# Two edits to a fused attention and feed-forward layer: attention and its output one head later, and the rotary halves swapped by VectorE instead of by DMA

## The chip, the cores and the metric

One Trainium2 chip, one core. The metric is the device time of one execution in microseconds (us). A profiled execution of the same program gives the trace.

## The reference

Input x is (4, 512, 512): four batches of 512 rows, 512 wide. The weights are integer codes with scales.

```
a = layernorm(x)
q, k, v = a @ Wq, a @ Wk, a @ Wv          # Wq = (codes - 8) * scales, 32 query heads, 8 key/value heads, 128 wide
q, k = rope(q), rope(k)                    # (even*cos - odd*sin, odd*cos + even*sin)
p = softmax(q k^T / sqrt(128) + causal mask)
x = x + layernorm((p v) @ Wo)              # each key/value head serves 4 query heads
x = x + layernorm(ffn(layernorm(x)))       # silu(gate) * up, then down; 1376 hidden
```

## The kernel before

All products run on TensorE (PE) in pairs or triples of float16 parts: a float32 value is written as high + low, and high*high, high*low and low*high are summed in PSUM. VectorE (DVE), ScalarE (ACT) and GpSimd (POOL) make those parts; the DMA queue that SyncE (SP) feeds turns matrices of parts by DMA transposes.

**Units and slots.** The attention part is 32 units (8 key/value heads times 4 batches), `UNITS`, and each unit is 4 slots, one per query head; head number n counts from 0 to 127. In a slot every engine goes through a list written out by hand in its own `unit` function, and the engines meet only at semaphores. In slot n, PE does, in this order (`unit` of the tensor block): `attend(n - 1)`, the product of probabilities and values of the head before (lines 843 to 845, 30 matmuls of 128 columns); the scores of head n + 1 in three groups (lines 827 to 829), with output tiles O0, O1, O2 of head n - 2 between them (lines 814 and 815); then the projections for the next unit that the table `FULL` gives this slot (K or Q0 to Q3, lines 790 to 792, 12 matmuls of 512 columns; V, lines 806 to 808, 48 of 128), and O3. So slots 0 and 1 of a unit carry two projections and slots 2 and 3 one.

**The ring.** Projections and output tiles share the four banks of `ps_p`; PE may refill a bank when DVE has emptied it (`bank_free`).

**DVE's slot.** Three times scaled, masked scores with their row minimum (line 1127) and the bias of the exponential (`bias`, line 1136), each followed by the addition of an output tile into y (`add_output`, line 1114); `invert` (line 1141); then `take` for each projection: the product with the sine table into `other` (line 1099) and with the cosine table into `rot` (line 1102), or V's low part (line 1091). Slot 1 has a `dequant` more (line 1058), slot 3 a `w_low` (line 1048).

**The other engines.** Of a rotary piece SP copies the two halves of `other` crosswise into `swap` by two DMAs (`swap_halves`, lines 370 and 371); POOL adds `swap` to `rot` (`rope_add`, line 492) and, after ACT's high part, makes the low one (`rope_low`, line 500). ACT does the exponentials (line 627) and the high parts of probabilities (line 636) and outputs (`o_norm`, lines 644 and 648); POOL their low parts (`p_low`, line 508; `o_low`, line 516). SP's list in a slot is: the swaps of the last slot's pieces, `turn_p_hi(n)`, `turn_p_lo(n)`, `turn_o(n - 1)` with two transposes (lines 395 and 398), then loads. Turned probabilities have two buffers: `turn_p_hi(n)` waits until head n - 2 has been attended (`oq_ps`).

**Around it.** A start makes the first unit's pieces in the order `START`; after unit 1, POOL issues the load of the feed-forward weights (lines 566 and 567); in the last unit the slots have turned rows (Y, X) in place of projections; behind it stand the last heads' attention and output, and then the feed-forward part.

Of the kernel before, what the change touches and what calls it, by code (L numbers as in the profile page):

```python
# [104 lines left out]
def outs_before(U):  # L105

    return HG * KT * U - 2 * KT
# [22 lines left out]


def swaps_landed(V, piece):


    users = BUF_USERS[ROPE_BUF[piece]]
    return 32 * (len(users) * V + users.index(piece) + 1)
# [21 lines left out]
def layer(nc, x, w_codes, w_scales, o_codes, o_scales,  # L158
          gate_t, gate_s, up_t, up_s, down_t, down_s, cos_t, sin_t, ident_in, mask_in, out):
    ctx = ExitStack()  # L160
    with ctx:
# [56 lines left out]
        other = sb("other", [P, 3, S], F32, att)  # L218
# [4 lines left out]
        o_hi = sb("o_hi", [P, S], F16, att)  # L223
        o_lo = sb("o_lo", [P, S], F16, att)
        ot_hi = sb("ot_hi", [P, 2, TT, P], F16, att)
        ot_lo = sb("ot_lo", [P, 2, TT, P], F16, att)
# [6 lines left out]
        inv_sum = sb("inv_sum", [P, 2, TT], F32, att)  # L233
# [44 lines left out]
        other_done = sem("other_done")  # L278
        swap_in = [sem("swap_in0"), sem("swap_in1"), sem("swap_in2")]
# [16 lines left out]
        ot_hi_in = sem("ot_hi_in")  # L296
        ot_lo_in = sem("ot_lo_in")
# [36 lines left out]
        def _(sp):  # L334
# [27 lines left out]
            def swap_halves(V, vpar, piece):  # L362


                buf = ROPE_BUF[piece]
                after(sp, rot_sum, buffer_before(V, piece))
                sp.sem_inc(sp_passed)
                sp.wait_ge(other_done, rope_index(V, piece) + 1)
                sp.sem_inc(sp_passed)
# [18 lines left out]
            def turn_o(n, hp):  # L388


                after(sp, o_ps, (n - 1) * KT)
                sp.sem_inc(sp_passed)
                sp.wait_ge(oq_hid, n + 1)
                sp.sem_inc(sp_passed)
# [21 lines left out]
            swap_halves(0, 0, "K")  # L416
            load_w(4, 0)
            swap_halves(0, 0, "Q0")
            load_w(5, 1)
            swap_halves(0, 0, "Q1")  # L420
            swap_halves(0, 0, "Q2")
# [7 lines left out]
            def unit(U, r, slots=FULL, first=False, more=True, last=False):  # L429
                for h in range(HG):  # L430
                    n = U * HG + h
                    if first and h == 0:
                        swap_halves(0, 0, "Q3")
                    else:
                        for V, vpar, piece, bank, taken in made_before(U, r, h, slots):
                            if piece != "V":
                                swap_halves(V, vpar, piece)
# [21 lines left out]
            unit(UNITS - 1, 1, slots=LAST, more=False, last=True)  # L459
            turn_o(UNITS * HG - 1, 1)  # L460
# [15 lines left out]
        def _(pool):  # L476
# [8 lines left out]
            def rope_add(V, vpar, piece, taken):  # L485
# [4 lines left out]
                pool.wait_ge(swap_in[buf], swaps_landed(V, piece))  # L490
                pool.sem_inc(pool_passed)
# [18 lines left out]
            def o_low(n):  # L510

                after(pool, ot_lo_in, 16 * n)
# [3 lines left out]
                pool.tensor_tensor(o_lo[:, :], o_f[:, :], o_hi[:, :], ALU.subtract).then_inc(oq_lod, 1)  # L516
# [25 lines left out]
            def unit(U, r, slots, last=False, first=False):  # L542
                for h in range(HG):
                    n = U * HG + h
                    p_low(n, h % 2)
                    if not (first and h == 0):
                        o_low(n - 1)
# [36 lines left out]
        def _(act):  # L584
# [103 lines left out]
            def unit(U, r, slots, last=False, first=False):  # L688
                for h in range(HG):
# [3 lines left out]
                    if not (first and h == 0):  # L693
                        o_norm(n - 1, (h - 1) % 2)
# [704 lines left out]
```

## Time and profile before

| | |
|---|---|
| time, median of 3 runs | 1589.76 us (1585.22 to 1591.85) |
| profiled execution: its own time | 1594.79 us |
| profiled execution: span of the trace | 1593.0 us |
| PE busy | 1440.8 us, 90% of the span |
| DVE busy | 1218.2 us, 76% |
| ACT busy | 936.1 us, 59% |
| POOL busy | 914.7 us, 57% |
| mean granted clock of TensorE | 0.978 of full speed |

The shares are means over a start, the 32 units and a feed-forward part, which have different limits; the 32 units take from about 61.5 us to 1347 us of the span. What an engine waited for has to be read by stretch.

### The profile page before, as it was taken

The numbers are of one execution on the slowest core, as the hardware profiler recorded it, in microseconds if no ns is written. First come the engines' busy times: TensorE is split into PE (matmuls) and PEld (weight loads), VectorE is DVE, ScalarE is ACT, GpSimd is POOL, SyncE is SP. The second block draws the span as 40 slices with busy tenths as digits, with TensorE's granted clock in tenths as the row PEclk, the third lists the DMA queues.
The fourth block names the chain that finished last, engine by engine and source line by source line (L and its number), as shares of the span: only waits on it lengthen the run. The fifth ranks groups of instructions, "written<-read, shape, count | busy, mean of one in ns | idle before, by whom it ended". The sixth has DMA issues, their size and how long they took to land.

```text
span 1593.0 us, 41176 instructions
## 1 busy us (share of the span) xinstructions
PE 1440.8 (90%) x11104; PEld 858.2 (54%) x11104; DVE 1218.2 (76%) x2884; ACT 936.1 (59%) x2198; POOL 914.7 (57%) x642
## 2 busy tenths in 40 slices
PE   5787898999999999998999999988999986999998
PEld 3454555556555555655555555555555553544543
DVE  7766688788878787877887888777878887776744
ACT  2555666667666666676666666666666763422411
POOL 3566676667766776776677667766676763110100
PEclk9999899999999999999999999999999998999999
DMA  7479888878787778877888788778778866010100
GB/s 241 95 154 179 165 161 158 151 153 159 153 154 153 158 156 145 159 158 152 150 161 165 151 150 160 156 150 152 147 161 156 153 140 122 14 53 21 34 27 27
DMA packets 526713, 217.17 MB, mean 136 GB/s; under 512 B 483041, under 2 KB 484801, under 8 KB 526529
## 3 DMA queue, kind: packets, MB, share of 16 engines
q1 hardware_dynamic: 524064, 210.54, 66.1%
q0 software_dynamic: 2464, 4.23, 1.6%
q8 instruction: 109, 1.79, 0.5%
q14 instruction: 76, 0.61, 0.1%
HBM read 55.32 MB, written 4.19 MB: 37 GB/s over the span
## 4 chain that ended last, share of the span: by engine, by line
PE 51%; issue 11%; DMA 10%; SPq 8%; DVE 7%; POOL 6%; ACT 5%; DVEq 1%; POOLq 0%; ACTq 0%
PE ps_p L792 4%; PE ps_p L790 4%; POOL p_lo L508 4%; PE ps_p L791 4%; PE ps_s L1023 4%; PE ps_s L1024 4%; PE ps_p L814 3%; DMA ot_lo<-o_lo 3%; PE ps_p L815 3%; PE ps_o L843 3%; PE ps_o L845 2%; PE ps_o L844 2%; PE ps_p L1037 2%; PE ps_p L1038 2%; PE ps_s L827 2%
## 5 line engine op out<-in xcount | busy, mean ns | idle before, releaser
L508 POOL TENSOR_TENSOR p_lo<-prob,p_hi 128x1280 f16<-128x1280 f32 x128 | 344.3, 2689 | 182.3 <-ACT p_hi L636 170.5
L1114 DVE SCALAR_TENSOR_TENSOR y<-ps_p,wo_scale,y 128x512 f32<-128x512 f32 x512 | 381.3, 746 | 73.9 <-PE ps_p L815 52.2
L627 ACT ACTIVATE prob<-prob,exp_bias 128x512 f32<-128x512 f32 (+3 forms) x512 | 283.3, 554 | 143.5 <-DVE exp_bias L1136 140.6
L843 PE MATMUL ps_o<-v_hi,ffn_w 128*128 128x128 f16 x1280 | 229.3, 223 | 95.2 <-issue 51.2
L1127 DVE CUSTOM_DVE_ANT_0 prob<-ps_s,mask 128x512 f32<-128x512 f32 (+3 forms) x512 | 238.0, 483 | 78.8 <-PE ps_s L829 78.5
L790 PE MATMUL ps_p<-x_hi,w_hi 128*128 128x512 f16 x640 | 244.9, 383 | 2.3 <-DVE x_lo L1082 1.4
L791 PE MATMUL ps_p<-x_lo,w_hi 128*128 128x512 f16 x640 | 244.7, 382 | 0.0
L792 PE MATMUL ps_p<-x_hi,w_lo 128*128 128x512 f16 x640 | 244.6, 382 | 0.0
L644 ACT ACTIVATE o_f<-ps_o,inv_sum 128x128 f32<-128x128 f32 x512 | 145.9, 368 | 150.4 <-PE ps_o L845 150.4
L845 PE MATMUL ps_o<-v_hi,ffn_w 128*128 128x128 f16 x1280 | 230.1, 224 | 0.0
L844 PE MATMUL ps_o<-v_lo,ffn_w 128*128 128x128 f16 x1280 | 229.7, 224 | 0.0
L492 POOL TENSOR_TENSOR rot<-rot,swap 128x512 f32<-128x512 f32 x160 | 202.4, 1272 | 18.0 <-DMA swap<-other 17.8
L516 POOL TENSOR_TENSOR o_lo<-o_f,o_hi 128x512 f16<-128x512 f32 x128 | 149.3, 1167 | 108.6 <-ACT o_hi L648 108.4
L814 PE MATMUL ps_p<-ot_hi,wo 128*128 128x512 f16 x512 | 195.8, 383 | 17.3 <-DMA ot_lo<-o_lo 15.7
L843 PEld LDWEIGHTS ps_o<-v_hi,ffn_w 128*128 128x128 f16 x1280 | 127.9, 100 | 132.7 <-issue 112.1
L815 PE MATMUL ps_p<-ot_lo,wo 128*128 128x512 f16 x512 | 195.7, 382 | 0.0
L500 POOL TENSOR_TENSOR q_lo<-rot,q_hi 128x512 f16<-128x512 f32 x128 | 148.3, 1169 | 70.0 <-ACT q_hi L613 69.9
L636 ACT ACTIVATE p_hi<-prob 128x1280 f16<-128x1280 f32 x128 | 162.6, 1271 | 15.2 <-DMA ffn_w<-p_hi 9.7
L539 POOL TENSOR_TENSOR rstd<-ve,minus_half 128x1 f32<-128x1 f32 x48 | 26.5, 551 | 244.5 <-DVE ve L1193 244.5
L1136 DVE TENSOR_SCALAR exp_bias<-low 128x1 f32<-128x1 f32 (+1 forms) x384 | 114.2, 297 | 64.9 <-DVE low L1127 11.1
L827 PE MATMUL ps_s<-k_hi,q_hi 128*128 128x512 f16 (+3 forms) x512 | 157.0, 307 | 7.4 <-POOL q_lo L500 4.0
L828 PE MATMUL ps_s<-k_lo,q_hi 128*128 128x512 f16 (+3 forms) x512 | 156.5, 306 | 0.0
(100 smaller groups left out, 2929.1 us busy)
## 6 DMA issues: line engine op xcount, KB each, us to landing
swap<-other SPq DMA_DIRECT2D x320, 128.0 KB, 3.1
w_code<-w_codes SPq DMA_DIRECT2D x36, 384.0 KB, 3.7
w_scale<-w_scales SPq DMA_DIRECT2D x36, 384.0 KB, 5.0
o_code<-o_codes SPq DMA_DIRECT2D x35, 256.0 KB, 3.0
swap<-x SPq DMA_DIRECT2D x16, 256.0 KB, 2.9
out<-z SPq DMA_DIRECT2D x16, 256.0 KB, 2.0
ffn_w<-x SPq DMA_DIRECT2D x3, 1024.0 KB, 9.7
ffn_w<-p_hi SPq DMA_TRANSPOSE x128, 3.7
```

What stands on the lines that cost most here:

```text
L508: pool.tensor_tensor(p_lo[:, :], prob[:, hp, :], p_hi[:, :], ALU.subtract).then_inc(p_lod, 1)
L627: act.activation(prob[:, hp, a:a + w], prob[:, hp, a:a + w], ACT.Exp, bias=exp_bias[:, hp, i:i + 1], scale=-1.0, accum_out=exp_sum[:, hp, ...
L790: pe.matmul(ps_p[:, bank, :], wh, xh, start=(k == 0), stop=False)
L791: pe.matmul(ps_p[:, bank, :], wh, xl, start=False, stop=False)
L792: mm = pe.matmul(ps_p[:, bank, :], wl, xh, start=False, stop=(k == KT - 1))
L814: pe.matmul(ps_p[:, bank, :], w, flat(ot_hi[:, hp, :, :]), start=True, stop=False)
L815: pe.matmul(ps_p[:, bank, :], w, flat(ot_lo[:, hp, :, :]), start=False, stop=True).then_inc(o_ps, 1)
L843: pe.matmul(o, ph, vh, start=(i == ORDER[0] and j == 0), stop=False)
L844: pe.matmul(o, ph, vl, start=False, stop=False)
L845: mm = pe.matmul(o, pl, vh, start=False, stop=(i == ORDER[-1]))
L1114: dve.scalar_tensor_tensor(tile, ps_p[:, bank, :], scale, tile, ALU.mult, ALU.add).then_inc(o_add, 1)
L1127: dve.tensor_tensor_reduce(prob[:, hp, P_AT[i]:P_AT[i] + w], ps_s[:, bank, col:col + w], mask[:, S - w:], -SCORE_SCALE, NO_MINIMUM, ALU.ad ...
```

## The change

1. **One head later.** PE, ACT, POOL and SP handle attention and output of head n - 2 in slot n, where they handled n - 1; output tiles are those of head n - 3. `inv_sum` gets four sets of columns for that. Two heads are left over behind the last slot, where one was.
2. **V moves.** K stands alone in slot 0, and V goes to slot 2 behind Q2; in the start it comes fifth.
3. **Merged transposes.** The high and low parts of an output lie side by side in `o_parts`, and one DMA transpose of 128x1024 turns both.
4. **Crosswise products.** The buffer `other` and the 320 swap DMAs are gone. DVE multiplies partitions 64 to 127 of the projection with the sine table and writes partitions 0 to 63 of `swap`, and then the other way round: two instructions of 64x512 where one of 128x512 stood.

```diff
-FULL = (("K", "V"), ("Q0", "Q1"), ("Q2",), ("Q3",))
+FULL = (("K",), ("Q0", "Q1"), ("Q2", "V"), ("Q3",))
-START = ("K", "V", "Q0", "Q1", "Q2", "Q3")
+START = ("K", "Q0", "Q1", "Q2", "V", "Q3")
...
-    return HG * KT * U - 2 * KT
+    return HG * KT * U - 3 * KT
...
-            def swap_halves(V, vpar, piece):
...
-                after(sp, rot_sum, buffer_before(V, piece))
-                sp.wait_ge(other_done, rope_index(V, piece) + 1)
-                sp.dma_start(swap[0:64, buf, :], other[64:128, buf, :]).then_inc(swap_in[buf], 16)
-                sp.dma_start(swap[64:128, buf, :], other[0:64, buf, :]).then_inc(swap_in[buf], 16)
...
                 after(sp, o_ps, (n - 1) * KT)
-                sp.wait_ge(oq_hid, n + 1)
-                sp.dma_start_transpose(ot_hi[:, hp, :, :], o_hi[:, :]).then_inc(ot_hi_in, 16)
                 sp.wait_ge(oq_lod, n + 1)
-                sp.dma_start_transpose(ot_lo[:, hp, :, :], o_lo[:, :]).then_inc(ot_lo_in, 16)
+                sp.dma_start_transpose(ot[:, hp, :, :], flat(o_parts[:, :, :])).then_inc(ot_in, 16)
...
                     turn_p_hi(n, h % 2)
                     turn_p_lo(n, h % 2)
-                    if not (first and h == 0):
-                        turn_o(n - 1, (h - 1) % 2)
+                    if not (first and h < 2):
+                        turn_o(n - 2, h % 2)
...
                 pool.wait_ge(piece_dve, taken)
-                pool.wait_ge(swap_in[buf], swaps_landed(V, piece))
                 pool.tensor_tensor(rot[:, buf, :], rot[:, buf, :], swap[:, buf, :], ALU.add).then_inc(rot_sum, 1)
...
                     p_low(n, h % 2)
-                        o_low(n - 1)
+                        o_low(n - 2)
...
-                        o_norm(n - 1, (h - 1) % 2)
+                        o_norm(n - 2, (h - 2) % HG)
...
-                    if h < 2:
-                        output(U - 1, HG - 2 + h, h, nt, bank_of(r, e))
+                    if h < 3:
+                        output(U - 1, h + 1, (h + 1) % 2, nt, bank_of(r, e))
...
-                    if h:
-                        attend(n - 1, r, (h - 1) % 2, pieces_before(U - 1) + START.index("V") + 1)
+                    if h > 1:
+                        attend(n - 2, r, h % 2, pieces_before(U - 1) + START.index("V") + 1)
...
-            attend(UNITS * HG - 1, (UNITS - 1) % 2, 1, 0)
+            attend(UNITS * HG - 2, (UNITS - 1) % 2, 0, 0)
...
-                last_output(HG - 2, nt, nt)
-            pe.wait_ge(o_add, outs - 2 * KT + 1)
+                last_output(1, nt, nt)
+            attend(UNITS * HG - 1, (UNITS - 1) % 2, 1, 0)
+            pe.wait_ge(o_add, outs - 3 * KT + 1)
...
                     dve.wait_ge(piece_ps, taken)
-                    after(dve, swap_in[buf], swaps_landed(V, piece) - 32)
+                    after(dve, rot_sum, buffer_before(V, piece))
-                    dve.tensor_tensor(other[:, buf, :], ps_p[:, bank, :], sin[:, :], ALU.mult).then_inc(other_done, 1)
+                    dve.tensor_tensor(swap[0:64, buf, :], ps_p[64:128, bank, :], sin[64:128, :], ALU.mult)
+                    dve.tensor_tensor(swap[64:128, buf, :], ps_p[0:64, bank, :], sin[0:64, :], ALU.mult)
                     after(dve, rot_lo, buffer_before(V, piece))
                     dve.tensor_tensor(rot[:, buf, :], ps_p[:, bank, :], cos[:, :], ALU.mult).then_inc(piece_dve, 1)
```

On DVE, slot 1 of the first unit, the slot with Q0 and Q1, reads as follows: before,

```order
L1141 RECIPROCAL inv_sum<-exp_sum 128x4
L1099 TENSOR_TENSOR other<-ps_p,sin 128x512
L1102 TENSOR_TENSOR rot<-ps_p,cos 128x512
L1099 TENSOR_TENSOR other<-ps_p,sin 128x512
L1102 TENSOR_TENSOR rot<-ps_p,cos 128x512
L1058 SCALAR_TENSOR_TENSOR w_scale<-w_code,w_scale 128x768
```

and with the change:

```order
L1109 RECIPROCAL inv_sum<-exp_sum 128x4
L1066 TENSOR_TENSOR swap<-ps_p,sin 64x512
L1067 TENSOR_TENSOR swap<-ps_p,sin 64x512
L1070 TENSOR_TENSOR rot<-ps_p,cos 128x512
L1066 TENSOR_TENSOR swap<-ps_p,sin 64x512
L1067 TENSOR_TENSOR swap<-ps_p,sin 64x512
L1070 TENSOR_TENSOR rot<-ps_p,cos 128x512
L1025 SCALAR_TENSOR_TENSOR w_scale<-w_code,w_scale 128x768
```

Each piece has three instructions in place of two, all ahead of the release of its bank.

On SP's queue, slot 2 of the first unit (slot 1 leaves two pieces to swap, and ends with the loads of codes and scales): before,

```order
L351 DMA w_scale<-w_scales 128x768
L370 DMA swap<-other 64x512
L371 DMA swap<-other 64x512
L370 DMA swap<-other 64x512
L371 DMA swap<-other 64x512
L380 DMA_TRANSPOSE ffn_w<-p_hi 128x10x128
L386 DMA_TRANSPOSE ffn_w<-p_lo 128x10x128
L395 DMA_TRANSPOSE ot_hi<-o_hi 128x4x128
L398 DMA_TRANSPOSE ot_lo<-o_lo 128x4x128
```

and with the change:

```order
L339 DMA w_scale<-w_scales 128x768
L357 DMA_TRANSPOSE ffn_w<-p_hi 128x10x128
L363 DMA_TRANSPOSE ffn_w<-p_lo 128x10x128
L372 DMA_TRANSPOSE ot<-o_parts 128x8x128
```

Six issues of such a slot have become three, and no issue of SP waits for a DVE product of a piece any more.

## Rows read from the trace of the kernel before

**Rows 1.** The page's first part: busy us, share of the span, instructions
```profile
PE 1440.8 (90%) x11104; PEld 858.2 (54%) x11104; DVE 1218.2 (76%) x2884; ACT 936.1 (59%) x2198; POOL 914.7 (57%) x642
```
**Rows 2.** Busy time by stretch: us, PE, PEld, DVE, ACT, POOL, PEclk, DMA share, GB/s
```profile
0.00:61.50 61.50, 34.25 (x184) 19.56 (x184) 49.76 (x97) 19.40 (x34) 22.57 (x22) 0.94 0.56 179
61.50:204.50 143.00, 120.94 (x988) 75.90 (x989) 95.90 (x243) 86.79 (x211) 88.11 (x60) 0.92 0.82 160
204.50:1187.80 983.30, 913.20 (x7702) 564.44 (x7701) 786.05 (x1925) 662.56 (x1601) 682.48 (x451) 0.99 0.80 155
...
1292.70:1347.20 54.50, 34.91 (x270) 22.82 (x271) 43.07 (x102) 26.39 (x63) 25.02 (x22) 0.87 0.61 119
```
**Rows 3.** Waits from 204.5 to 1187.8 us: us in total, times, longest
```profile
DVE prob L1127 <- PE ps_s L829: 59.5, 66, 2.1
...
PE ps_o L843 <- issue: 44.9, 39, 2.6
DVE y L1114 <- PE ps_p L815: 44.8, 49, 1.9
...
DVE other L1099 <- PE ps_p L792: 19.7, 18, 1.3
PE ps_p L814 <- DMA ot_lo<-o_lo: 13.7, 11, 2.1
```
**Rows 4.** PE's timeline at 806.5 us: start us, duration us
```profile
806.50 0.22 PE L843 MATMUL ps_o<-v_hi,ffn_w 128*128 128x128 f16 x1
806.56 0.22 PE L844 MATMUL ps_o<-v_lo,ffn_w 128*128 128x128 f16 x1
...
806.89 0.38 PE L828 MATMUL ps_s<-k_lo,q_hi 128*128 128x512 f16 x1
807.10 0.38 PE L829 MATMUL ps_s<-k_hi,q_lo 128*128 128x512 f16 x1
```
**Rows 5.** DVE's groups from 204.5 to 1187.8 us: busy us, mean ns, idle us before
```profile
L1102 DVE TENSOR_TENSOR rot<-ps_p,cos 128x512 f32<-128x512 f32 x125 | 84.7, 678 | 0.0
L1099 DVE TENSOR_TENSOR other<-ps_p,sin 128x512 f32<-128x512 f32 x125 | 83.3, 666 | 21.7 <-PE ps_p L792 19.7 <-issue 0.5
...
L1136 DVE TENSOR_SCALAR exp_bias<-low 128x2 f32<-128x2 f32 x100 | 60.1, 601 | 17.2 <-DVE low L1127 3.2
...
L1136 DVE TENSOR_SCALAR exp_bias<-low 128x1 f32<-128x1 f32 x200 | 30.8, 154 | 34.1 <-DVE low L1127 6.2
```
**Rows 6.** DVE's timeline at 814 us, a piece being taken
```profile
814.07 0.17 DVE L1141 RECIPROCAL inv_sum<-exp_sum 128x4 f32<-128x4 f32 x1
814.15 0.66 DVE L1099 TENSOR_TENSOR other<-ps_p,sin 128x512 f32<-128x512 f32 x1
814.73 0.68 DVE L1102 TENSOR_TENSOR rot<-ps_p,cos 128x512 f32<-128x512 f32 x1
815.32 0.74 DVE L1114 SCALAR_TENSOR_TENSOR y<-ps_p,wo_scale,y 128x512 f32<-128x512 f32 x1
```
**Rows 7.** DVE's timeline at 1320 us, the second waiting for the first
```profile
1319.93 0.69 DVE L1211 TENSOR_TENSOR y<-y,swap 128x512 f32<-128x512 f32 x1
1320.65 0.69 DVE L1191 BATCH_NORM_STATS2 stats<-y 128x6 f32<-128x512 f32 x1
```
**Rows 8.** DVE's timeline at 820.7 us
```profile
820.66 0.76 DVE L1136 TENSOR_SCALAR exp_bias<-low 128x2 f32<-128x2 f32 x1
```
**Rows 9.** POOL's timeline at 820.1 us
```profile
820.14 1.26 POOL L492 TENSOR_TENSOR rot<-rot,swap 128x512 f32<-128x512 f32 x1
```
**Rows 10.** The page's DMA issues: median us from issue to landing
```profile
swap<-other SPq DMA_DIRECT2D x320, 128.0 KB, 3.1
...
ffn_w<-p_hi SPq DMA_TRANSPOSE x128, 3.7
```
**Rows 11.** Busy time from 150 to 165 us, columns as in rows 2
```profile
150.00:165.00 15.00, 3.55 (x51) 3.06 (x49) 2.49 (x6) 3.26 (x7) 3.13 (x3) 0.67 1.09 193
```
**Rows 12.** PE's waits from 1292.7 to 1347.2 us
```profile
PE ps_o L843 <- DMA ffn_w<-p_lo: 13.9, 5, 5.0
```

More of the change, by code:

```diff
@@ L431, in unit @@
                     n = U * HG + h
[L432 to L437, printed above, removed]
                     turn_p_hi(n, h % 2)
                     turn_p_lo(n, h % 2)
-                    if not (first and h == 0):
-                        turn_o(n - 1, (h - 1) % 2)
+                    if not (first and h < 2):
+                        turn_o(n - 2, h % 2)
                     if first:
@@ L510, in o_low @@
             def o_low(n):
-                after(pool, ot_lo_in, 16 * n)
+                after(pool, ot_in, 16 * n)
                 pool.sem_inc(pool_passed)
@@ L545, in unit @@
                     p_low(n, h % 2)
-                    if not (first and h == 0):
-                        o_low(n - 1)
+                    if not (first and h < 2):
+                        o_low(n - 2)
                     if first and h == 0:
@@ L572, in _ @@
             unit(UNITS - 1, 1, LAST, last=True)
+            o_low(UNITS * HG - 2)
+            power(2 * TT - 1)
             o_low(UNITS * HG - 1)
-            power(2 * TT - 1)
             full = (FT - 1) * P
@@ L644, in o_norm @@
                     act.activation(o_f[:, i * P:(i + 1) * P], ps_o[:, i * P:(i + 1) * P], ACT.Copy,
-                                   scale=inv_sum[:, hp, i:i + 1]).then_inc(oq_norm, 1)
-                after(act, ot_hi_in, 16 * n)
+                                   scale=inv_sum[:, h, i:i + 1]).then_inc(oq_norm, 1)
+                after(act, ot_in, 16 * n)
                 act.wait_ge(oq_norm, (n + 1) * TT)
-                act.activation(o_hi[:, :], o_f[:, :], ACT.Copy).then_inc(oq_hid, 1)
+                act.activation(o_hi, o_f[:, :], ACT.Copy).then_inc(oq_hid, 1)
             def rows_out(t, bank):
@@ L692, in unit @@
                         o_centre(h)
-                    if not (first and h == 0):
-                        o_norm(n - 1, (h - 1) % 2)
+                    if not (first and h < 2):
+                        o_norm(n - 2, (h - 2) % HG)
                     if h == 3 and not last:
@@ L813, in output @@
                 w = flat(by_half(wo)[:, bass.ds((U >> 2) & 1, 1), h, nt * P:(nt + 1) * P])
-                pe.matmul(ps_p[:, bank, :], w, flat(ot_hi[:, hp, :, :]), start=True, stop=False)
-                pe.matmul(ps_p[:, bank, :], w, flat(ot_lo[:, hp, :, :]), start=False, stop=True).then_inc(o_ps, 1)
+                pe.matmul(ps_p[:, bank, :], w, flat(ot[:, hp, 0:TT, :]), start=True, stop=False)
+                pe.matmul(ps_p[:, bank, :], w, flat(ot[:, hp, TT:2 * TT, :]), start=False, stop=True).then_inc(o_ps, 1)
             def scores(n, U, upar, h, g):
@@ L883, in unit @@
                 names = sequence(slots)
-                idle = place(slots, 2, "O0") if first else 0
+                idle = place(slots, 3, "O0") if first else 0
                 def bank_free(e):
@@ L913, in out_tile @@
                 def out_tile(n, h, nt):
-                    if first and h < 2:
+                    if first and h < 3:
                         return
@@ L918, in out_tile @@
                     if nt == 0:
-                        pe.wait_ge(ot_hi_in, 16 * (n - 1))
-                        pe.wait_ge(ot_lo_in, 16 * (n - 1))
-                    if h < 2:
-                        output(U - 1, HG - 2 + h, h, nt, bank_of(r, e))
+                        pe.wait_ge(ot_in, 16 * (n - 2))
+                    if h < 3:
+                        output(U - 1, h + 1, (h + 1) % 2, nt, bank_of(r, e))
                     else:
                         if first:
-                            pe.wait_ge(o_cent, h - 1)
-                        elif b == 0 and h == 2 and nt == 0:
+                            pe.wait_ge(o_cent, 1)
+                        elif b == 0 and nt == 0:
                             pe.wait_ge(o_cent, U + HG)
-                        output(U, h - 2, h - 2, nt, bank_of(r, e))
+                        output(U, 0, 0, nt, bank_of(r, e))
                 for h in range(HG):
@@ L1238, in out_tile @@
                     before = outs_before(U) + h * KT + nt
-                    if h > 1:
-                        add_output(U, b, h - 2, nt, bank, before)
+                    if h > 2:
+                        add_output(U, b, 0, nt, bank, before)
                     elif not first:
-                        add_output(U - 1, (b - 1) % NB, HG - 2 + h, nt, bank, before)
+                        add_output(U - 1, (b - 1) % NB, h + 1, nt, bank, before)
                 for h in range(HG):
@@ L1295, in _ @@
             xn_low(TT - 1, ps_p[:, 1, :])
-            for nt in range(KT):
-                add_last(HG - 1, nt, (nt + 2) % RING)
+            for h in (2, 3):
+                for nt in range(KT):
+                    add_last(h, nt, (nt + 2) % RING)
             dve.wait_ge(sc_cv, 4)
```

65 lines of the change are left out of this document (26 added, 39 removed).

## The prediction

> **What bounds the kernel now.** I read the page's busy shares first: PE is at 90% of the span and DVE at 76% [rows 1]. Shares hide the stages, so the table by stretch comes next [rows 2]. From 204.5 to 1187.8 us lie 25 equal units: 983.3 us, 39.33 us each. PE is busy in 913.2 us of them, DVE in 786.05, POOL in 682.48, ACT in 662.56. PE stands for 70.1 us, 2.8 us a unit, and the list of waits says where: 44.9 us ahead of the first matmul of `attend` (line 843) and 13.7 us ahead of output tile O0, which waits for the turned outputs [rows 3]. "Issue" names no releaser, but that matmul waits for turned probabilities and values alone, so I take these 44.9 us for the transposes. DVE in turn waits for PE in three places, 59.5, 44.8 and 19.7 us: 124.0 us, 4.96 us a unit [rows 3]. Nobody is saturated; two engines wait for each other and for a long chain between them.
>
> What would each need by itself? **PE:** matmuls start 0.21 us apart at 512 columns and 0.055 us apart at 128 [rows 4]. A unit has 5 x 12 projection matmuls, 32 of output tiles and 12 of scores at 512 columns, 104 x 0.214 = 22.3 us; 12 each of scores at 384 and 256, by columns 3.2 us; and 120 + 48 + 12 at 128, 180 x 0.055 = 9.9 us. That is 35.4 us; busy time gives 913.2 / 25 = 36.5 us with matmuls at the lower clock in it. I take 35.8. **DVE:** busy 786.05 / 25 = 31.4 us, plus 51.3 us / 25 = 2.05 us of idle ahead of the biases, which wait for the row minimum made just before [rows 5]: 33.5 us at least. At most it is 39.33 - 4.96 = 34.4 us, all that is not a wait for PE. I take 34.0. So PE limits, and the change can win 39.3 - 35.8 = 3.5 us a unit if nothing else grows.
>
> **The change, part by part.**
>
> *One head later.* `attend` of a head gets a slot more, 9.8 us on the mean, for its transposes. The longest wait ahead of line 843 is 2.6 us [rows 3], so in the equal units these waits go. The turned probabilities have two buffers, so that SP can turn head n only when PE has attended n - 2, which now comes one slot later; after that 3.7 us to landing [rows 10] leave over a slot. Output tiles keep their distance from their attention (one slot), so this move alone doesn't free the 13.7 us. The merged transpose saves one SP issue in that chain, and the swaps in front of it are gone: I count the 13.7 us as gone too, half of it being worth 0.3 us a unit if I am wrong. V in slot 2 makes PE's slots K, Q0+Q1, Q2+V, Q3, and gives POOL and ACT, which handle Q0 and Q1 in slot 2, a long slot for it. These edits cost nothing of any engine's work.
>
> *No swap DMAs.* POOL no longer waits for 3.1 us of transfer per piece [rows 10]. On PE's or DVE's path it was not: I count 0.
>
> *Crosswise products.* This is the price. A piece now takes three DVE instructions where it took two. An instruction of 128x512 on that data takes 666 to 678 ns [rows 5], and its time is set by the 512 elements of a partition, so half the partitions save nothing that a row shows. Between zero and a full one, I take a full one. In a row of independent instructions the next starts 0.58 to 0.59 us after the one before, ahead of its end [rows 6]; where one must wait for the other, they start 0.72 us apart, 0.03 us behind the end [rows 7]. Which of the two holds here no row tells: every DVE instruction of this trace lies at partition 0, while the new ones read from 64 and write to 0, then the reverse, and `rot` goes back to 0. Lower bound for a piece: one more start at 0.59 us. Upper: also three starts (both crosswise products and `rot`) pushed from 0.59 to 0.72, 0.59 + 3 x 0.13 = 0.98 us. I take 0.93, close to the upper end, because the overlap is shown for instructions alike in their partitions only. Five pieces: +4.65 us a unit, bounds +2.95 and +4.9.
>
> The Trainium skill ("VectorE: DVE Perf Modes", section "Two Vector instructions with no wait between them") speaks against the change here: an instruction whose input or output starts in another group of 32 partitions than the last one from or into that memory starts only when all earlier ones have finished. By it all three starts are held and the upper end holds. No row here shows it.
>
> *Sum for equal units.* DVE needs 34.0 + 4.65 = 38.65 us, PE 35.8. DVE becomes the bound. PE can run four banks ahead, and it is 2.9 us a unit faster, so DVE waits for it no more: 38.65 us, -0.65 to -0.7 us a unit. Over the 27.7 units between 204.5 and 1292.7 us: **-18 us**.
>
> *Start.* Up to 61.5 us DVE is busy in 49.8 us [rows 2] and sets the pace; four or five pieces at +0.93: +4. From 61.5 to 204.5 us, 143.0 us for 13 slots, DVE is busy in 95.9 only: waits for transposes prevail, among them the stretch from 150 to 165 us, in which the load of feed-forward weights fills the DMA engines (share 1.09) and PE works 3.55 us of 15 [rows 11]. After: 3.25 units at 38.65 = 125.6 us, less 12 output additions that the first three slots don't have (0.67 each, 8 us), plus that stall, of which a head of slack saves little, since the output transposes sit behind the same queue: 11 us; plus 2 for slots without full lead. 131 us: -12. Together: **-8 us**.
>
> *End.* In the last unit PE waits 13.9 us for turned probabilities [rows 12], but DVE is busy in 43.1 of 54.5 us [rows 2], and the second left-over head adds four additions (2.7 us) and its attention behind the last slot. I take -4 + 3: **-1 us**. The feed-forward part is untouched.
>
> Sum: -18 - 8 - 1 = -27 us against the profiled execution's 1594.8 us: 1567.8. That execution lies 5.0 us over the median of 1589.76, so the forecast is **1563 us**.
>
> **Rivals.**
>
> 1. *The new instructions overlap like the old ones.* Then a piece costs +0.59 us. DVE needs 34.0 + 2.95 = 36.95, with 0.3 for two engines nearly level 37.3 us a unit: -2.0 x 27.7 = -55; the start gains 1.7 x 3.25 + 1.6 = 7 more, -15; the end -1. 1594.8 - 71 - 5.0 = **1519 us**. For it: starts before the end are the rule in this trace [rows 6]. Against it: all those rows work on the same partitions.
>
> 2. *The biases are held behind POOL (slower).* The bias of two columns takes 0.60 us on the mean, that of one column 0.15 [rows 5], and in the example it starts at 820.66 and ends at 821.42, with POOL's addition, which ends at 821.40 [rows 8, 9]. When DVE never catches up, its place beside POOL's list moves, and each of the four a unit may hit a POOL instruction for 1.1 us: +2.0 us a unit. 38.65 + 2.0 = 40.65, +1.3 x 27.7 = +36; the start -1, the end -1: **1624 us**. It decides from 0.17 us per such bias, where a unit is at 39.3 again. For it: POOL is busy in 69% of the stretch. Against it: it was busy as often before, so the mean of 0.60 should hold. The Trainium skill ("SBUF — State Buffer", section "Who interferes with whom") has such a lock on a shared port, for two-port modes and for two SBUF inputs; the new products have one SBUF input and would be free of it.
>
> 3. *The gain is given back in small change:* DVE at the upper ends (34.4 + 4.9 = 39.3) with the start's -8 alone, or PE still waiting for outputs: 1582 to 1590, **1585 us**. That the attention isn't freed at all, because the two buffers hold the transposes back, would end here as well; the 3.7 us to landing speak against it.
>
> **How the numbers follow.** About 0.5% (7.9 us) is what a measurement of this kernel can tell from no change. Forecast case 0.55, mostly 1545 to 1583, so 0.47 of it over 0.5% faster and 0.08 within; rival 1 0.25, all faster; rival 3 0.10, 0.07 within and 0.03 beyond; rival 2 0.10, slower. Faster 0.72, the same 0.15, slower 0.13. The range must reach rival 1: 1512 leaves out some 0.07 of its lower side, and 1590 leaves out 0.13 above.
>
> **What the profile would show.** If right: waits ahead of the attention's matmul near zero in the equal units; DVE busy over 90% there, its waits for PE under 1 us a unit; PE waiting for banks that DVE empties; the unit at 38.4 to 38.9 us; crosswise products of some 0.67 to 0.69 us that start 0.7 us apart. Starts 0.6 us apart and units of 37.3 us mean rival 1. A mean over 0.77 us for the bias of two columns means rival 2. It is wrong altogether if DVE is still idle for 3 us a unit or more waiting for PE, or if `attend` still waits.

## The result: 1619 us, 1.7% slower, and the profile after

The changed kernel takes **1619.42 us** (median of 4 runs, 1617.21 to 1620.76); the kernel before, on the same chip, 1590.8 us (4 runs, one more than the 1589.76 us had). The ratio is 1.0172, with a 95% interval of 1.0121 to 1.0223. The forecast was 1563 us, with a range of 1512 to 1590: wrong in its sign, and outside its range. The profiled execution took 1617.21 us, 22.4 us over the one before. Two executions far off the rest, 2147.84 us in `crosswise_bias_on_scalar` and 3016.85 us in `before_w_low_early`, enter no ratio below; without them these two medians would be 1524.00 and 1596.57 us.

First the page: busy us, share, instructions, and the engines of the chain that ended last.

```profile
PE 1457.8 (90%) x11104; PEld 853.1 (53%) x11104; DVE 1385.9 (86%) x3044; ACT 930.6 (58%) x2198; POOL 938.4 (58%) x642
...
DVE 31%; PE 30%; issue 23%; DMA 5%; DVEq 4%; POOL 4%; ACT 2%; SPq 1%; POOLq 0%; ACTq 0%
```

DVE is busy for 167.7 us more than in [rows 1]. The 160 pieces at the forecast's 0.93 us are at most 149 of them, since 0.93 us was a price from start to start, with idle time in it; 19 us or more are something else. The table by stretch says where the time is (columns as in rows 2):

```profile
0.00:66.80 66.80, 33.98 (x184) 20.10 (x185) 53.62 (x101) 19.62 (x34) 22.79 (x22) 0.92 0.44 149
66.80:200.50 133.70, 114.56 (x902) 69.52 (x903) 106.50 (x247) 82.00 (x200) 86.12 (x57) 0.92 0.72 137
200.50:1197.00 996.50, 927.42 (x7702) 560.17 (x7701) 916.96 (x2049) 657.18 (x1598) 702.43 (x450) 0.99 0.64 120
1276.40:1369.50 93.10, 68.35 (x556) 43.52 (x555) 78.35 (x181) 50.69 (x124) 48.51 (x38) 0.90 0.65 116
```

The first three stretches hold the same work as the first three of [rows 2]. 61.5 us have become 66.8, 143.0 have become 133.7, and the 25 equal units 996.5 us after 983.3: **39.86 us a unit after 39.33**, with DVE busy 36.7 us of each (31.4 before). The last stretch is the end: its like took 81.9 us before (1265.3 to 1347.2). So of the 22.4 us the start gives -4.0, the 27 equal units in all +15.1, the end +11.3.

The waits from 200.5 to 1197.0 us (in total, times, longest) are to be set beside [rows 3]:

```profile
PE ps_o L808 <- DMA ffn_w<-p_lo: 20.6, 6, 3.6
...
PE ps_p L779 <- DVE rot L1070: 16.4, 19, 1.1
...
PE ps_p L779 <- DVE y L1082: 12.1, 24, 1.1
PE ps_p L779 <- DMA ot<-o_parts: 8.0, 13, 1.2
...
DVE prob L1095 <- PE ps_s L794: 4.5, 5, 1.2
```

DVE waited for PE 124.0 us before; 4.5 us at this line and 1.5 at `y` are left. PE now waits for banks that DVE should have emptied. The attention's matmul (now line 808) waits in 6 places, where it had waited in 39 for "issue" alone. That is the picture that the forecast had drawn, yet with a unit that is 1.2 us longer than drawn. DVE's groups in the stretch (busy us, mean ns, idle before), beside [rows 5]:

```profile
L1066 DVE TENSOR_TENSOR swap<-ps_p,sin 64x512 f32<-64x512 f32 x125 | 86.6, 693 | 3.9
L1070 DVE TENSOR_TENSOR rot<-ps_p,cos 128x512 f32<-128x512 f32 x125 | 86.4, 691 | 1.7
L1067 DVE TENSOR_TENSOR swap<-ps_p,sin 64x512 f32<-64x512 f32 x125 | 85.5, 684 | 1.7
...
L1104 DVE TENSOR_SCALAR exp_bias<-low 128x2 f32<-128x2 f32 x100 | 62.7, 627 | 14.9
L1015 DVE SCALAR_TENSOR_TENSOR w_lo<-w_scale,w_hi 128x768 f32 x25 | 58.7, 2347 | 0.0
```

The bias of two columns, which rival 2 feared for, went from 601 to 627 ns: next to nothing. The new item is `w_lo`, DVE's part of `w_low`, which the forecast never priced. Before, it stood at

```profile
L1048 DVE SCALAR_TENSOR_TENSOR w_lo<-w_scale,w_hi 128x768 f32 x25 | 30.7, 1229 | 0.0
```

with a median of 942 ns and three of 3.3 to 3.4 us; now it takes 2.35 us in **each** of the 25 units. DVE's and POOL's timelines show why. Of the changed kernel, with the last bias of the slot first:

```profile
829.21 0.17 DVE L1104 TENSOR_SCALAR exp_bias<-low 128x2 f32<-128x2 f32 x1
...
831.88 2.62 POOL L471 TENSOR_TENSOR p_lo<-prob,p_hi 128x1280 f16<-128x1280 f32 x1 [1.41 <-ACT p_hi L600]
...
832.96 2.35 DVE L1015 SCALAR_TENSOR_TENSOR w_lo<-w_scale,w_hi 128x768 f32 x1
834.45 1.87 POOL L479 TENSOR_TENSOR o_parts<-o_f,o_parts 128x512 f16<-128x512 f32 x1
```

Of the kernel before, two slots of the same kind:

```profile
784.15 2.62 POOL L508 TENSOR_TENSOR p_lo<-prob,p_hi 128x1280 f16<-128x1280 f32 x1 [1.16 <-ACT p_hi L636]
784.29 3.29 DVE L1048 SCALAR_TENSOR_TENSOR w_lo<-w_scale,w_hi 128x768 f32 x1
...
823.91 0.94 DVE L1048 SCALAR_TENSOR_TENSOR w_lo<-w_scale,w_hi 128x768 f32 x1
824.42 2.91 POOL L508 TENSOR_TENSOR p_lo<-prob,p_hi 128x1280 f16<-128x1280 f32 x1 [1.02 <-ACT p_hi L636]
```

Where `w_lo` starts half a microsecond ahead of POOL's `p_lo` it takes 0.94 us, and `p_lo` takes 0.3 more. Where it starts 0.14 us behind it, it takes 3.29: it sits through nearly all of `p_lo` and only then works. In the changed kernel it starts 1.08 us behind `p_lo`, which ends at 834.50, and ends itself 0.81 us after that, at 835.31; POOL's next operation then takes 1.87 us where it takes 1.16 elsewhere. The Trainium skill ("SBUF — State Buffer", "Who interferes with whom") says that a VectorE instruction with two SBUF inputs contends with a GpSimd instruction that reads SBUF, and that issue order decides who blocks; the three cases above agree with both. The forecast cited that very section for the biases and overlooked that `w_lo` has two SBUF inputs.

It is the same in every unit because both starts follow from one event, the end of the slot's last bias. `p_lo` follows it by 2.5 to 3.0 us (exponentials, high part), and `w_lo` follows it by what stands between them in DVE's list. Before, `w_lo` came 2.49 us behind that end and `p_lo` 2.99 in 17 of the 25 units, all of them units whose last bias had itself taken more than 0.3 us; where the bias took 0.17 to 0.20 us, `w_lo` came after 2.6 us and `p_lo` after 2.5 to 3.0, and the three long ones are among these eight. Now, with one product more between, `w_lo` comes after 3.6 us and `p_lo` after 2.5, every time.

### The profile page after: what moved, and what is told of

It is laid out like the page before. It is cut to its first block, busy times and chain, and to the rows that moved or that the text cites. A ratio compares the mean times of both kernels' runs of the same rounds, so it can differ in the third digit from the quotient of the medians.

```text
span 1615.4 us, 40014 instructions
## 1 busy us (share of the span) xinstructions
PE 1457.8 (90%) x11104; PEld 853.1 (53%) x11104; DVE 1385.9 (86%) x3044; ACT 930.6 (58%) x2198; POOL 938.4 (58%) x642
## 4 chain that ended last, share of the span: by engine, by line
DVE 31%; PE 30%; issue 23%; DMA 5%; DVEq 4%; POOL 4%; ACT 2%; SPq 1%; POOLq 0%; ACTq 0%
DVE prob L1095 9%; DVE y L1082 5%; PE ps_s L990 4%; PE ps_s L991 4%; DVE w_lo L1015 3%; DVE swap L1066 3%; DVE rot L1070 2%; DVE w_scale L1025 2%; POOL p_lo L471 2%; PE ps_p L1005 2%; PE ps_p L1004 2%; DMA ffn_w<-p_lo 2%; PE ps_p L779 2%; DVE swap L1067 2%; PE ps_p L780 2%
## 5 line engine op out<-in xcount | busy, mean ns | idle before, releaser
L471 POOL TENSOR_TENSOR p_lo<-prob,p_hi 128x1280 f16<-128x1280 f32 x128 | 335.8, 2623 | 201.6 <-ACT p_hi L600 197.4
L779 PE MATMUL ps_p<-ot,wo 128*128 128x512 f16 x512 | 199.9, 390 | 76.8 <-DMA ot<-o_parts 33.0
L808 PE MATMUL ps_o<-v_hi,ffn_w 128*128 128x128 f16 x1280 | 227.9, 223 | 21.5 <-DMA ffn_w<-p_lo 20.6
L455 POOL TENSOR_TENSOR rot<-rot,swap 128x512 f32<-128x512 f32 x160 | 218.4, 1373 | 5.5 <-DVE rot L1070 5.5
L780 PE MATMUL ps_p<-ot,wo 128*128 128x512 f16 x512 | 199.2, 389 | 0.0
L479 POOL TENSOR_TENSOR o_parts<-o_f,o_parts 128x512 f16<-128x512 f32 x128 | 166.5, 1301 | 30.3 <-ACT o_parts L612 29.6
```

The source lines that it names most:

```text
L471: pool.tensor_tensor(p_lo[:, :], prob[:, hp, :], p_hi[:, :], ALU.subtract).then_inc(p_lod, 1)
L779: pe.matmul(ps_p[:, bank, :], w, flat(ot[:, hp, 0:TT, :]), start=True, stop=False)
L780: pe.matmul(ps_p[:, bank, :], w, flat(ot[:, hp, TT:2 * TT, :]), start=False, stop=True).then_inc(o_ps, 1)
L808: pe.matmul(o, ph, vh, start=(i == ORDER[0] and j == 0), stop=False)
```

## The experiments

**Theory 1:** DVE is now the bound, so whatever it is held for behind POOL is paid in full; the crosswise products cost what was forecast, and the holds come on top. **Theory 2:** the merged transposes, or PE's waits for them, bound the later schedule. Each unit length below is the distance between two starts of the attention 25 units apart, divided by 25. The experiments ran in three batches; beside them the kernel before took 1593.05, 1596.68 and 1594.73 us, and each ratio is to its own batch's.

### Swap DMAs back: the later head without the crosswise products

```diff
-                    dve.tensor_tensor(swap[0:64, buf, :], ps_p[64:128, bank, :], sin[64:128, :], ALU.mult)
-                    dve.tensor_tensor(swap[64:128, buf, :], ps_p[0:64, bank, :], sin[0:64, :], ALU.mult)
+                    dve.tensor_tensor(other[:, buf, :], ps_p[:, bank, :], sin[:, :], ALU.mult).then_inc(other_done, 1)
```

and `swap_halves` in SP's list and POOL's wait for it as before.

> The changed kernel with the swap DMAs and the one 128x512 product put back; the later attention, V in slot 2 and the merged transposes stay. Theory 1 (VectorE is the bound of the changed kernel, at some 39.5 us a unit, of which the crosswise products are 4.7 and waits behind POOL 1.3): without the products VectorE needs about 34 us, PE 35.8 plus the restart of its loop every fourth unit (3.4 us), so units of 36.5 to 37.2 us and 1520 to 1545 us in all, faster than both kernels. Theory 2 (the later attention itself costs, by longer chains or transposes): no faster than before, 1585 us or more.

Measured: 1575.77 us, ratio to before 0.9899 (0.9862 to 0.9936). The direction was right, the size about half: 43.7 us below the changed kernel, where 74 to 99 were expected. The unit is 38.34 us, though DVE's instructions are those of before. Their time is not (groups from 204 to 1180 us, busy us, mean ns):

```profile
L1048 DVE SCALAR_TENSOR_TENSOR w_lo<-w_scale,w_hi 128x768 f32 x25 | 75.0, 3000 | 0.0
L1136 DVE TENSOR_SCALAR exp_bias<-low 128x2 f32<-128x2 f32 x102 | 72.4, 710 | 15.2
L1058 DVE SCALAR_TENSOR_TENSOR w_scale<-w_code,w_scale 128x768 f32<-128x768 int32 x26 | 72.1, 2772 | 0.0
```

Against 1229, 601 and 1475 ns before, that is 1.77 + 4 x 0.11 + 1.30 = 3.5 us a unit more in holds. Here is one, DVE's and POOL's timeline:

```profile
803.37 2.61 POOL L504 TENSOR_TENSOR p_lo<-prob,p_hi 128x1280 f16<-128x1280 f32 x1 [1.03 <-ACT p_hi L633]
803.50 3.29 DVE L1048 SCALAR_TENSOR_TENSOR w_lo<-w_scale,w_hi 128x768 f32 x1
```

`w_lo` is 0.13 us too late. Another 0.9 us a unit is a new wait, for the high part of V in slot 2, which the changed kernel doesn't have (DVE's waits from 204 to 1180 us):

```profile
DVE v_lo L1091 <- ACT v_hi L616: 23.5, 25, 2.1
```

34.0 + 3.5 + 0.9 is 38.4 us. The 34.0 us that the forecast took for DVE's own time hold only for the schedule they were read from.

### Crosswise products alone, in the kernel before

The same three lines the other way round, and nothing else of the change.

> The kernel before with the crosswise products alone in place of the swap DMAs. Theory 1 (VectorE bound): VectorE's own 34.0 + 4.7 = 38.7 us a unit is near the 39.3 of before, where it also waited 5 us a unit for PE; PE's waits for transposes stay, the two add in part: 40.5 to 42 us a unit, 1625 to 1670 us. Theory 2 (the products ride in VectorE's idle time, and the loss comes from the later attention): 1585 to 1600 us.

Measured: 1624.27 us, ratio 1.0208 (1.0167 to 1.0249), unit 40.1 us. The crosswise products are thus what makes the changed kernel slow; beside them the later head wins back 5 us, within the intervals. PE still waits ahead of its attention here, 48.4 + 17.8 us from 204 to 1180 us. `w_lo` took 2611 ns.

### `w_low` ahead of the pieces

```diff
                     invert(n, h)
+                    if h == 3 and not last:
+                        w_low(U + 5)
...
-                    if h == 3 and not last:
-                        w_low(U + 5)
```

> The changed kernel with the low part of the weights (w_low, 2.35 us each in the changed kernel, 1.23 before) placed ahead of the piece of slot 3, when POOL stands idle, and not behind the last output tile, when POOL starts p_low. Theory 1 (it is held until POOL's instruction ends): 0.95 to 1.3 us each, units 1 us shorter, 1585 to 1600 us. Theory 2 (it is slow by itself, or a stall only moves to the next instruction): the same 1619 us within 5.

Measured: 1587.86 us, 31.6 us less than the changed kernel; ratio to before 0.9965 (0.9939 to 0.9992). One instruction of DVE's list has moved, 31 times in the kernel, and the loss against the kernel before is gone:

```profile
L1015 DVE SCALAR_TENSOR_TENSOR w_lo<-w_scale,w_hi 128x768 f32 x25 | 26.0, 1041 | 0.0
```

2347 - 1041 = 1.3 us, 31 times, is 40 us of holds (an estimate, with the mean of the equal units for all 31), and 32 of them show in the time. The unit is 38.74 us, 0.1 over the 38.65 us of the forecast.

### Two products of 128 partitions at partition 0

```diff
+                    dve.tensor_tensor(swap[:, buf, :], ps_p[:, bank, :], sin[:, :], ALU.mult)
+                    dve.tensor_tensor(other[:, buf, :], ps_p[:, bank, :], sin[:, :], ALU.mult)
```

in place of the two crosswise ones. This kernel leaves out the swapping of the halves, so its result is not the layer's.

> The changed kernel with two products of 128x512 at partition 0 in place of the two crosswise ones; the swapping of the halves is left out. Three VectorE instructions per piece as in the changed kernel, none of them from or to partition 64. Theory 1 (what costs beyond the third instruction is that instructions which start at other partitions may not overlap): starts 0.58 to 0.60 us apart, a piece at 1.79 in place of 2.13 us, 1.7 us a unit less, 1565 to 1585 us. Theory 2 (three instructions cost the same wherever they lie): starts 0.70 us apart, 1619 us.

Measured: 1576.39 us (one run). The three instructions of a piece, and the `y` behind them, in the changed kernel:

```profile
801.95 0.17 DVE L1109 RECIPROCAL inv_sum<-exp_sum 128x4 f32<-128x4 f32 x1
802.15 0.69 DVE L1066 TENSOR_TENSOR swap<-ps_p,sin 64x512 f32<-64x512 f32 x1
802.86 0.68 DVE L1067 TENSOR_TENSOR swap<-ps_p,sin 64x512 f32<-64x512 f32 x1
803.55 0.69 DVE L1070 TENSOR_TENSOR rot<-ps_p,cos 128x512 f32<-128x512 f32 x1
804.16 0.74 DVE L1082 SCALAR_TENSOR_TENSOR y<-ps_p,wo_scale,y 128x512 f32<-128x512 f32 x1
```

and with two plain products:

```profile
799.19 0.16 DVE L1110 RECIPROCAL inv_sum<-exp_sum 128x4 f32<-128x4 f32 x1
799.28 0.66 DVE L1067 TENSOR_TENSOR swap<-ps_p,sin 128x512 f32<-128x512 f32 x1
799.86 0.68 DVE L1068 TENSOR_TENSOR other<-ps_p,sin 128x512 f32<-128x512 f32 x1
800.45 0.68 DVE L1071 TENSOR_TENSOR rot<-ps_p,cos 128x512 f32<-128x512 f32 x1
801.05 0.74 DVE L1083 SCALAR_TENSOR_TENSOR y<-ps_p,wo_scale,y 128x512 f32<-128x512 f32 x1
```

From the reciprocal's start to that of `y` there are 2.21 us crosswise, 1.86 plain, and 1.25 in the kernel before with one product less [rows 6]. The piece costs 0.96 us more than before (forecast: 0.93): 0.61 for an instruction, 0.35 for three held starts.

### Two straight halves

```diff
+                    dve.tensor_tensor(swap[0:64, buf, :], ps_p[0:64, bank, :], sin[0:64, :], ALU.mult)
+                    dve.tensor_tensor(swap[64:128, buf, :], ps_p[64:128, bank, :], sin[64:128, :], ALU.mult)
```

This kernel leaves out the swapping too.

> The changed kernel with its two products of 64 partitions reading and writing the same half (0 to 0, then 64 to 64), so the halves are not swapped and the rotation is left out of the result. If a product is held because it reads or writes at another start partition than the one ahead of it, the second product and the one with cos are still held (starts 0.69 apart) and only the first one's hold goes: at most 0.12 us x 5 a unit, 1600 to 1617 us. If crossing from one half to the other is what costs, or nothing but crossing is held, all three start 0.59 apart: 1576 to 1590 us, as two_plain_products.

Measured: 1586.43 us, ratio 0.9946 (0.9926 to 0.9967). By its time alone it would be the crossing that costs. The timeline says otherwise:

```profile
804.05 0.16 DVE L1109 RECIPROCAL inv_sum<-exp_sum 128x4 f32<-128x4 f32 x1
804.14 0.65 DVE L1066 TENSOR_TENSOR swap<-ps_p,sin 64x512 f32<-64x512 f32 x1
804.80 0.69 DVE L1067 TENSOR_TENSOR swap<-ps_p,sin 64x512 f32<-64x512 f32 x1
805.51 0.69 DVE L1070 TENSOR_TENSOR rot<-ps_p,cos 128x512 f32<-128x512 f32 x1
806.12 0.74 DVE L1082 SCALAR_TENSOR_TENSOR y<-ps_p,wo_scale,y 128x512 f32<-128x512 f32 x1
```

The first product starts 0.09 us behind the reciprocal, not held; the next two start 0.66 and 0.71 us apart, right behind the end of the one before: held, though neither crosses from one half to the other. What they have in common with the crosswise ones is another start partition than the instruction before. The Trainium skill ("VectorE: DVE Perf Modes", "Two Vector instructions with no wait between them") says that an instruction is held when an input or its output starts in another group of 32 partitions than the last one from or into that memory; the free start and the two held ones here agree. The piece gains 0.14 us, 0.7 us a unit; the unit fell by more, from 39.90 us by this measure to 38.81, because `w_scale` fell to 988 ns from 1536, while `w_lo` rose to 2490 from 2347: 0.70 + 0.55 - 0.14 = 1.1 us. With DVE saturated, each small edit shifts which instruction meets POOL, and the time moves by more than the edit. That made this run's time a poor witness.

### Swap DMAs and the early `w_low` together

> The changed kernel with the swap DMAs and the one product of 128 partitions back, and the low part of the prepared weight made right behind the reciprocal of slot 3 instead of behind its fourth y add. Theory 1 (VectorE is the bound, and what it loses is time held behind GpSimd): with the swap DMAs the two weight operations still took 3.00 and 2.77 us where free ones take 0.94 and 0.95; with the first at its free price VectorE's unit falls from about 37.9 to 35.9 us, TensorE's 36.5 us and its waits decide, about 37.3 us a unit, 25 to 30 us off 1575.8: 1551 us (1542 to 1562). Theory 2 (the merged transposes, which reach TensorE late, bound the later schedule; its waits for ot were 0.78 us a unit): VectorE's time is no matter, 1572 to 1580 us.

Measured: **1538.77 us**, ratio 0.9655 (0.9606 to 0.9704), 37 us below the same kernel with `w_low` in its old place, more than expected. `w_lo` now takes 1306 ns, `w_scale` 1413 (2772), the bias of two columns 408 (710). DVE's other held instructions, which nobody touched, became shorter as well. That isn't a rule: with still more room on DVE, in `swap_dmas_bias_on_scalar` below, `w_scale` takes 2127 ns again. The unit is 37.1 us.

### The biases on ScalarE

```diff
-                dve.tensor_scalar(exp_bias[:, hp, first:first + count], low[:, hp, first:first + count], EXP_UP, None,
-                                  ALU.add).then_inc(bias_done, 1)
...
+                act.wait_ge(low_done, n * TT + DONE[g])
+                act.activation(exp_bias[:, hp, first:first + count], low[:, hp, first:first + count], ACT.Copy,
+                               bias=EXP_UP).then_inc(bias_done, 1)
```

at the head of `exps`, with the early `w_low`. First with the crosswise products, then with the swap DMAs.

> The changed kernel, crosswise products kept, with the early low part of the weight (as in w_low_before_the_pieces, 1587.9 us) and the twelve small bias additions of a unit done by ScalarE instead of VectorE. Theory 1: VectorE loses 4 x 0.61 + 8 x 0.154 us of work and 1.8 us of waiting for its own reductions, 5.4 us a unit, ScalarE (26 us busy of 38.7) gains some 2 to 3; VectorE is then at about 33 us, TensorE is the bound with 36.9 us and its loop restarts, about 37.5 us a unit: 1588 - 1.2 x 28 = 1554 us (1545 to 1565), and the crosswise products cost nothing any more. Theory 2 (transposes and DMA): 1580 us or more.

> As crosswise_bias_on_scalar, but with the swap DMAs and the one product of 128 partitions back. Theory 1: neither has VectorE as its bound, so the two come out within 0.5% of each other, about 1551 us (1540 to 1562). Theory 2 (what the swap DMAs take from the transposes counts once VectorE is free): slower than the crosswise one by 8 us or more. If VectorE's 4.65 us a unit still counted, this one would be faster by 8 us or more.

Measured: **1524.26 us** crosswise, ratio 0.956 (0.9499 to 0.9621); **1529.86 us** with the swap DMAs, 0.9591 (0.9543 to 0.9639). The 64 us below `w_low_before_the_pieces` are twice what was expected. Crosswise the unit is 36.6 us on the mean, with most units at 35.8 to 36.2, and nearly all that PE waits for in the equal units is one place in sixteen slots (from 204 to 1180 us):

```profile
PE ps_o L812 <- DVE rot L1074: 12.6, 6, 2.2
...
PE ps_p L783 <- DMA ot<-o_parts: 0.5, 2, 0.2
```

Here DVE is busy 30.5 us of a unit crosswise and 27.7 with the DMAs, and neither decides. Crosswise or DMA was a matter of 31 us in the kernel before and of 44 in the later schedule (1619.42 and 1575.77); now it is 6 us, the other way round and within the intervals. What made the products dear was an engine without room.

### The same edits in the kernel before

The early `w_low` alone, then with the biases on ScalarE.

> The kernel before with one edit: the low part of the prepared weight right behind the reciprocal of slot 3, as in w_low_before_the_pieces. Theory 1 (what counts is whether VectorE ever catches up: only then do its held operations fall at other places): before, VectorE still waits for TensorE several times a unit and the operation took 1.23 us on the mean, so the move is worth 0 to 0.3 us a unit: 1583 to 1593 us. Theory 3 (the place of this operation alone made both orders slow, the move is worth as much as the 37 us between later_with_swap_dmas and swap_dmas_and_w_low): 1555 to 1565 us.

> The kernel before with the early low part of the weight and the biases on ScalarE: what the later head is worth once VectorE is not the bound. Theory 1: VectorE is at about 28 us, but TensorE still waits ahead of attend for the transposes of p, which nothing covers in the old order (before 1.3 to 2.0 us in two or three slots of four); with the shorter way from the minima to the exponentials some of it goes: 37.5 to 38.5 us a unit, 1550 to 1575 us, behind swap_dmas_bias_on_scalar (1529.9) by 20 us or more. Rival: the later head was worth nothing and the VectorE edits did it all: within 8 us of 1530.

Measured: 1596.89 us, ratio 1.0014 (0.9988 to 1.004): nothing that the runs can tell, as theory 1 had it; there `w_lo` was mostly free already (1229 ns on the mean, 1074 with the move). Then 1584.65 us, 0.9944 (0.9918 to 0.9969), less than expected: DVE is at 27.0 us a unit and waits for PE, and PE waits for its transposes as before (204 to 1180 us):

```profile
PE ps_o L847 <- issue: 37.5, 39, 2.0
PE ps_p L818 <- DMA ot_lo<-o_lo: 16.7, 13, 2.2
PE ps_o L847 <- DMA ffn_w<-p_lo: 8.5, 6, 1.6
```

So the later head, with V's move and the merged transposes, is worth 1584.65 - 1529.86 = 55 us once DVE has room, and 17 us (1593.05 to 1575.77) with its list as it was. Theory 2 is out: once DVE has room, the merged transposes hold nobody in the equal units.

### The end: the down load behind the last transpose

```diff
-            pool.wait_ge(oq_ps, UNITS * HG)
+            pool.wait_ge(ot_in, 16 * UNITS * HG)
             pool.dma_start(down_w[:, 0:FT - 1, :], ...
```

> The changed kernel with one edit at its end: GpSimd issues the load of the down weights only when the last transpose of the output parts has landed. Theory 1 (the last transpose takes 7.7 us because it is queued behind that load): it lands within 3 to 4 us of its issue, TensorE's last wait for ot falls from 4.4 us to under 1 us, and the time falls by 3 to 5 us, to 1614 to 1617 us. Theory 2 (these waits are the length of the chain attend, norm, parts, transpose, with nothing left to cover it): the wait keeps 3 us or more and the time is within 1 us of the changed kernel's.

Measured: 1615.67 us, 3.75 below the changed kernel. The intervals of the two ratios overlap, so the time alone doesn't show it, but the timeline does. Of the changed kernel:

```profile
1356.01 1.02 POOL L541 DMA_DIRECT2D ffn_w<-down_t  x1
1356.16 1.23 SPq L372 DMA_TRANSPOSE ot<-o_parts  x1
...
1364.08 0.58 PE L779 MATMUL ps_p<-ot,wo 128*128 128x512 f16 x1 [4.42 <-DMA ot<-o_parts]
```

and with the edit:

```profile
1357.52 1.23 SPq L372 DMA_TRANSPOSE ot<-o_parts  x1
...
1360.69 0.38 PE L779 MATMUL ps_p<-ot,wo 128*128 128x512 f16 x1 [0.98 <-DMA ot<-o_parts]
```

From issue to the matmul it is 7.9 us behind the load and 3.2 ahead of it. Two waits of 3.2 and 3.9 us for `ot` stay. I put them down to the length of the chain from attention to turned output, with nothing left to cover it; no run tests that.

### All edits, and PE's loop written out

```diff
-            with pe.Fori(0, UNITS // NB - 1) as p:
+            for p in range(0, UNITS // NB - 1):
```

> crosswise_bias_on_scalar with the down load after the last transpose, and TensorE's loop over four units written out, so that its queue has no branch. Theory 1 (a restart of TensorE's loop costs 2.1 to 3.5 us of instructions that arrive late, 7 times, and the down load 3 to 4 us once): no gap over 1 us ahead of attend at slots 22, 38, 54, and so on, every unit of the loop 35.8 to 36.2 us, 1524.3 - 7 x 2.2 - 3.5 = 1505 us (1500 to 1512). Rival: straight code is fetched from memory just as late, and the gaps spread over the units: 1518 to 1525 us.

Measured: **1501.91 us** (1500.61 to 1506.53), ratio 0.9424 (0.9398 to 0.945), the fastest version run. The page, and PE's waits from 204 to 1180 us:

```profile
PE 1420.9 (95%) x11104; PEld 855.9 (57%) x11104; DVE 1197.8 (80%) x2660; ACT 990.6 (66%) x2582; POOL 906.8 (60%) x642
```

```profile
PE ps_p L783 <- DVE y L1086: 2.0, 4, 0.6
PE ps_p L783 <- DMA ot<-o_parts: 2.0, 3, 1.2
```

The gap ahead of the attention in every sixteenth slot is gone. It was 3.3 to 3.6 us in the changed kernel (the 6 waits of 20.6 us above), stood at the point where PE's loop over four units starts anew, and was put down to a transpose or to `rot`, whichever came last. With it and the down load 22.4 us are gone. In the 25 equal units, which hold the restarts, of which there are six, not the seven of the expectation, it is 36.58 - 35.97 us a unit, 15.2 us or 2.5 us a restart; no run parts the rest into the load and something else. In `crosswise_bias_on_scalar` the six units with a restart took 38.0 to 39.7 us, the others mostly 35.8 to 36.2. The Trainium skill ("Runtime: NRT & Kernel Launch", "Instruction fetch mechanics") says that a taken branch to a page outside the two at hand has to wait until that page is fetched. The traces agree: at each of the six restarts of `crosswise_bias_on_scalar` queue q8, which the page of the profile calls instruction, has two loads of 16 KB 3.2 to 3.3 us apart, and with the loop written out no two lie closer than 8.7 us. Units are 35.97 us, with PE busy 35.8 of them: the 35.8 us of the forecast's sum.

## Why the prediction was wrong

- **What bounds the kernel, PE's 35.8 us.** Right, and reached exactly in the last experiment. It left out the restart of PE's loop: 20.6 us of waits in 25 units of the changed kernel, most of it made up for in the unit behind (41.8 us, then 38.6, in most cases, where the others take 39.8). In the kernel before, PE stood for 1.1 to 1.6 us at the same six places, no longer than at others, so nothing pointed at them.
- **One head later.** Right: the 44.9 us ahead of the attention went, apart from the restarts; of the 13.7 us for turned outputs 8.0 stayed. It is worth 55 us once DVE has room. (In the slot that was shown of SP's list eight issues have become three, not six.)
- **Crosswise products, +0.93 us a piece.** Right: 0.96. So was the reading of the rule on held starts, which no row then at hand showed.
- **"DVE needs 34.0 + 4.65 = 38.65 us".** This is the step that failed. 34.0 us was read from a schedule in which `w_lo` mostly passed ahead of `p_lo`, and taken for a property of DVE's list. Moved behind it, `w_lo` costs 2.35 us for 1.23 in each unit. 38.65 + 1.12 for `w_lo`, 0.06 for `w_scale` and 0.10 for the biases is 39.9 us, and 39.86 was measured. Instead of -18 us the units gave +15.1; and with `w_low` put ahead of the pieces they are at 38.7. That kernel's 1588 us are still 25 over the forecast: the misses of 4 and 12 us at start and end, below, stand in it as well.
- **Rival 2** had the mechanism, the sign and the point of decision (over 39.3 us a unit), but the wrong instruction. It put it on the biases, for which "the mean of 0.60 should hold" proved true. Its chance of 0.10 was too small: DVE's list holds three kinds of instruction that come in long and short here (`w_lo`, `w_scale`, the bias of two columns), and only one was looked at. That its 1624 us lie near the 1619 measured is luck: it had 2.0 us a unit in the biases and -1 at the end, and it was 1.3 us, nearly all in `w_lo`, and +11.3 at the end.
- **The start, -8.** -4.0: up to the first slot +5.3 for +4; the 13 slots behind it -9.3 for -12.
- **The end, -1.** +11.3. The waits for probabilities went, as foreseen (13.9 us, [rows 12]), but 13.2 us of waits for `ot` took their place. Two heads' outputs are now left over behind the last slot, and the down load stands ahead of the last one's transpose, which costs some 4 us. The sum had priced their additions and not the chain that leads to them; how the other 7 us or so divide no run shows.

All told -27 was forecast and +22.4 came: 33 of the difference of 49 us lie in the units, 12 in the end, 4 in the start.

## What to carry to other kernels

An engine's busy time is no constant where another engine can hold its instructions. Before adding work to an engine that would become the bound, list its instructions whose durations come in two sizes (here 0.94 and 3.3 us), note how far each starts from the other engine's long instruction, and work out where the added work moves it: here a lead of 0.5 us that became a lag of 1.1 us was worth 32 us. The cheapest cure here was to move one such instruction ahead, the strongest to give small work to an engine whose instructions took the same time throughout (185 to 206 ns on ACT).

A saturated engine makes edits look larger or smaller than they are. The crosswise products cost 31 us in the kernel before and 44 with DVE full, and nothing that the runs can tell when it had room.

## What was not expected

- Small edits free more than themselves. Moving `w_low` was worth 0 us in the kernel before, 32 in the changed one and 37 with the swap DMAs, where `w_scale` fell from 2.77 to 1.41 us and the biases from 0.71 to 0.41 without being touched.
- Twelve additions of one or two columns a unit, moved to ACT (188 ns each there), took 64 us off `w_low_before_the_pieces`. On DVE they cost 3.7 us of busy time and 1.8 us of waiting for the row minima, and up to 1.1 us each where they met POOL.
- A DMA transpose that was issued 0.15 us behind a load of weights from another queue was used 7.9 us after its issue, and 3.2 us after it when it went first.
- What stays open: how much of the 64 us is room on DVE and how much is the shorter way from the minima to the exponentials; no run parts them.
